# Router scores taken from the out-projection's own columns, normed rows on ScalarE, and a new order of the first expert tile

## The reference

```python
h = concat([tokens(x), txt], axis=1)              # (4, 384, 192)
# block: xn = layernorm(h); xz = xn @ in_proj_w.T; conv of 4 taps, silu -> u
#   dt = softplus(u @ dt_w.T + dt_b); state = exp(dt*A)*state + dt*B*u  (16 states); y = sum_n C_n*state_n
#   r = (y + D*u) * silu(z) @ out_w.T + xn
h = h + (r - mean(r)) / sqrt(var(r) + 1e-5) * ln_g + ln_b
# experts: xf = layernorm(h)
router_logits = xf @ Wr.T                         # 8 experts
topk_vals, topk_idx = top_k(router_logits, 2); w = softmax(topk_vals)
h = h + sum_k w_k * (gelu(xf @ Wi[e_k].T + bi[e_k]) @ Wo[e_k].T + bo[e_k])
```

## Time and profile before

| | us |
|---|---|
| median of 3 runs | 439.72 (438.59 to 440.37) |
| profiled execution | 440.68, of which the span 438.9 |
| TensorE busy | 375.9 (86%), mean granted clock 0.92 |
| VectorE busy | 275.1 (63%) |
| Pool busy | 224.3 (51%) |
| ScalarE busy | 197.8 (45%) |

### The profile page before, as it was taken

One profiled execution on the slowest core, in us unless ns is written; L12 is line 12 of the kernel. 1 busy time (PEld: TensorE's weight loads), 2 busy tenths in 40 slices (PEclk: granted clock), 3 DMA queues, 4 the chain that ended last, 5 costly groups with the idle time before them and its releaser, 6 DMA issues.

```text
span 438.9 us, 6787 instructions
## 1 busy us (share of the span) xinstructions
PE 375.9 (86%) x2247; PEld 281.5 (64%) x2247; DVE 275.1 (63%) x498; ACT 197.8 (45%) x502; POOL 224.3 (51%) x166
## 2 busy tenths in 40 slices
PE   5989897989849968879688698899999999999960
PEld 4546555644425535545355586699999999999960
DVE  4525479899899999999995566343443534435300
ACT  1455576566915565445550210135444454444420
POOL 6777732666546727576370003035565564655421
PEclk9998999799979978999699866699999999999995
DMA  6310015544637764989664411313323233233314
GB/s 174 67 12 4 7 24 132 120 114 125 136 92 233 239 219 144 261 236 292 182 184 175 197 37 41 127 23 54 56 43 56 48 51 54 42 55 50 38 21 117
DMA packets 36614, 46.97 MB, mean 107 GB/s; under 512 B 8877, under 2 KB 25214, under 8 KB 36014
## 3 DMA queue, kind: packets, MB, share of 16 engines
q1 hardware_dynamic: 29262, 38.94, 30.9%
q0 software_dynamic: 7328, 7.74, 11.7%
HBM read 40.65 MB, written 7.19 MB: 109 GB/s over the span
## 4 chain that ended last, share of the span: by engine, by line
PE 49%; DVE 17%; POOL 8%; DMA 7%; issue 6%; SPq 6%; ACT 4%; POOLq 0%; DVEq 0%; ACTq 0%
PE ps L1106 14%; PE ps L1089 10%; PE ps L1095 6%; DVE w_all L1620 5%; POOL w_all L664 4%; PE ps L852 4%; DMA w_all<-bc_dram 4%; SPq L530 3%; DVE ps L1612 3%; POOL w_all L614 2%; DMA sum_dram<-u_cm,tok_row 2%; DVE y_cm L1566 2%; PE ps L1079 2%; PE ps L919 2%; SPq L528 1%
## 5 line engine op out<-in xcount | busy, mean ns | idle before, releaser
L664 POOL TENSOR_TENSOR w_all<-w_all 128x768 f32<-128x768 f32 x47 | 78.9, 1680 | 73.0 <-DVE w_all L1620 27.4
L689 POOL DMA_INDIRECT sum_dram<-u_cm,tok_row x31 | 50.3, 1622 | 65.9 <-ACT u_cm L1441 59.5
L919 PE MATMUL ps<-w_all,cst 128*128 128x512 f32 x96 | 56.8, 675 | 22.5 <-POOL w_all L664 22.2
L1620 DVE TENSOR_TENSOR_SCAN w_all<-decay,ps 128x780 f32<-128x780 f32 x40 | 71.1, 1779 | 1.5 <-POOL w_all L664 0.2
L673 POOL DMA_INDIRECT dt_cm<-x_dram,tok_in x31 | 30.6, 986 | 51.4 <-DVE decay L1790 37.2
L614 POOL DMA_INDIRECT w_all<-in_pix,gidx x42 | 45.1, 1074 | 14.8 <-issue 12.5
L852 PE MATMUL ps<-cst 128*128 128x256 f32 x136 | 41.2, 463 | 5.6 <-DMA cst<-in_cst 5.0
L1426 ACT ACTIVATE u_cm<-ps,x_cm 128x128 f32<-128x128 f32 x96 | 26.6, 377 | 42.2 <-PE ps L1095 42.2
L1612 DVE TENSOR_TENSOR ps<-dtu_cm,ps 128x768 f32<-128x768 f32 x40 | 38.0, 949 | 2.9 <-PE ps L900 1.6
L919 PEld LDWEIGHTS ps<-w_all,cst 128*128 128x128 f32 x96 | 17.4, 208 | 34.3 <-POOL w_all L664 30.1
L852 PEld LDWEIGHTS ps<-cst 128*128 128x128 f32 x136 | 30.5, 232 | 13.4 <-DMA cst<-in_cst 5.0
(11 more groups left out here) (228 smaller groups left out, 686.4 us busy)
## 6 DMA issues: line engine op xcount, KB each, us to landing
w_all<-bc_dram SPq DMA_DIRECT2D x48, 256.0 KB, 3.6
w_all<-bc_dram SPq DMA_DIRECT2D x96, 64.0 KB, 3.7
w_all<-in_w_all SPq DMA_DIRECT2D x20, 289.0 KB, 4.2
w_all<-in_w_all SPq DMA_DIRECT2D x3, 1156.0 KB, 7.4
b_wide_sb<-bc_dram SPq DMA_DIRECT2D x8, 256.0 KB, 3.9
x_dram<-x_cm SPq DMA_DIRECT2D x3, 384.0 KB, 5.1
sum_dram<-h_tok SPq DMA_DIRECT2D x3, 384.0 KB, 3.5
out<-sum_dram SPq DMA_DIRECT2D x4, 288.0 KB, 3.8
```

Source lines behind the costliest of these rows:

```text
L664: nc.gpsimd.tensor_tensor(segments(hcs[at % 2]), inner(states[at % 2]), segments(c_sb[at % RING]), ALU.mult).then_inc(hc_rdy, 1)
L689: pool.indirect_dma_start(sum_dram, bass.IndirectOffsetOnAxis(ap=tok_row[:, i:i + 1].bitcast(U32), axis=0), y_out[:, i % 2, :], None, comp ...
L919: nc.tensor.matmul(sums[:, 0:4 * P], ident, hcs[at % 2][:, 0:4 * P], start=False, stop=at % S == S - 1, skip_group_check=True)
L1620: v.tensor_tensor_scan(states[p], fade, drive, 0.0, ALU.mult, ALU.add).then_inc(scanned, 1)
```

## The change

The last norm of a token is of h = h0 + (r - mean)*g/dev + b. Its shift and scale do not change which experts are largest. So the scores are built from parts: the router's weights less their mean over channels (`w_rt`, `w_b`), times g; the input's part (`token_rows`, from the transposed normed input), and the out-projection with 8 further columns that hold out_w times those weights (`mixed_weights`); `unscaled_scores` and `router_scores` put them together behind the first deviation alone. Only the difference of the two best is later scaled by the second deviation for the softmax. `router_rows` of VectorE, the transposes and logit matmuls of TensorE and ScalarE's copies for them go; ScalarE makes the normed rows in one instruction per tile from a scale and a shift (`row_shift`). The last chunk's out-projection goes to four banks and is signalled in two halves; new h and its statistics come behind the count. The gates are made behind the slots. Fillers are counted anew. Of the first expert tiles, the transposes of tile 1, the copies of weights and the stores' additions change order. The six added loads bring g and b with one channel per partition. The core of the diff:

```diff
+        N_TOK, N_IN, N_MIX = 11, 3, 12
         JS = [2, 0, 1]
 
         RUNS = [(2 * P + K - 1, L), (0, P), (P, 2 * P + K - 1)]
         NORMS = [(0, 2), (0, 0), (0, 1), (1, 0), (2, 0), (1, 1), (2, 1), (1, 2), (2, 2)]
-        WARM = {"input weights": 10, "coarse levels": 2, "fine patches": 4, "patches": 7, "normed rows": 7, "convolution": 2,
-                "first step": 12, "router's rows": 14, "counts": 6, "slots": 9, "bias rows": 2,
-                "first tile": 3}
+        WARM = {"input weights": 10, "coarse levels": 2, "fine patches": 2, "patches": 7, "normed rows": 7, "convolution": 2,
+                "first step": 10, "last rows": 11, "slots": 20, "bias rows": 1, "first tile": 4}
...
+        def attn_bank(j, b):
+            return 4 * (b % 2) + b // 2 if j == NJ - 1 else 4 + b // 2
+
+        def attn_rows(j, b):
+            at = 0 if j == NJ - 1 else 256 * (b % 2)
+            return ps[:, attn_bank(j, b), at:at + C + E]
...
+            by_channel = d["ln_gb"].rearrange("o g c -> c o g")
+            for k in range(2):
+                sp.dma_start(gb_c[:, 0, k:k + 1], by_channel[0:P, :, k]).then_inc(ld_mix, 16)
+                for half in range(2):
+                    sp.dma_start(gb_c[CB * half:CB * half + CB, 1, k:k + 1], by_channel[P:C, :, k]).then_inc(ld_mix, 16)
...
-                if at in (1, 5, 9):
-                    add_shift(at // 4)
+                if at in (1, 5, S + 2):
+                    add_shift(at // 4 if at < S else 2)
...
+            def router_weights():
+
+                pe.wait_ge(ld_mix, 16 * N_MIX)
+                pe.wait_ge(ones_set, 1)
+                pe.wait_ge(z_ready, 1)
+                nc.tensor.matmul(ps[:, 6, 0:E], ones_p, wr[:, 0, :], start=True, stop=False)
+                nc.tensor.matmul(ps[:, 6, 0:E], ones_p[0:CB, :], wr[0:CB, 1, :], start=False, stop=True)\
+                    .then_inc(w_sum_ps, 1)
+                for at, c in ((0, slice(0, P)), (256, slice(P, C))):
+                    o = ps[0:c.stop - c.start, 7, at:at + C]
+                    nc.tensor.matmul(o[:, 0:P], ow[:, 0, c], ident, start=True, stop=True)
+                    mm = nc.tensor.matmul(o[:, P:C], ow[0:CB, 1, c], ident[0:CB, 0:CB], start=True, stop=True)
+                mm.then_inc(owt_ps, 1)
+
+            def token_rows(n, bank, at):
+
+                for i in range(2):
+                    o = ps[:, bank, at + 4 * E * i:at + 4 * E * i + 4 * E]
+                    for half in range(2):
+                        b = 2 * half + i
+                        nc.tensor.matmul(o[:, 2 * E * half:2 * E * half + 2 * E], xt_a[:, P * b:P * b + P], w_rt[:, 0, :],
+                                         start=(half == 0), stop=False, skip_group_check=True)
+                    mm = nc.tensor.matmul(o, xt_b[:, P * i:P * i + P], w_two[:, :, :].rearrange("p h e -> p (h e)"),
+                                          start=False, stop=True, skip_group_check=True)
+                mm.then_inc(rows_ps, 1)
+
+            def first_rows():
+
+                pe.wait_ge(w_rt_step, 6)
+                pe.wait_ge(abs_rdy, 1)
+                pe.wait_ge(linear_rdy, 1)
+                for at, lo, hi in ((0, w_rt[:, 0, E:2 * E], w_rt[0:CB, 1, E:2 * E]), (E, w_b[:, 0, :], w_b[0:CB, 1, :])):
+                    nc.tensor.matmul(ps[:, 5, at:at + E], ones_p, lo, start=True, stop=False)
+                    nc.tensor.matmul(ps[:, 5, at:at + E], ones_p[0:CB, :], hi, start=False, stop=True)
+                token_rows(0, 5, 64)
+
+            def mixed_weights():
+
+                attn_free(0)
+                pe.wait_ge(owt_rdy, 1)
+                for o, ch in ((ps[:, 5, 0:E], slice(0, P)), (ps[0:CB, 5, E:2 * E], slice(P, C)),
+                              (ps[CB:P, 5, E:2 * E], slice(P, C))):
+                    nc.tensor.matmul(o, owt_a[:, ch], w_rt[:, 0, E:2 * E], start=True, stop=False)
+                    mm = nc.tensor.matmul(o, owt_b[:, ch], w_rt[0:CB, 1, E:2 * E], start=False, stop=True)
+                mm.then_inc(mixed_ps, 1)
...
             z_projection(0, 6)
             coarse_transposes()
-            keep_warm(WARM["coarse levels"], 4)
+            router_weights()
             coarse_levels()
-            pe.wait_ge(ld_mix, 16 * N_MIX)
             pe.wait_ge(x_out, 2)
             dt_low(0)
             dt_high_and_bc(0)
             coarse_rows()
             keep_warm(WARM["fine patches"], 0)
+            first_rows()
...
+            pe.wait_ge(abs_rdy, 3)
+            pe.wait_ge(linear_rdy, 3)
+            token_rows(1, 4, 0)
...
+            def last_residual_rows(i):
+
+                if i:
+                    attn_free(2)
+                else:
+                    pe.wait_ge(scanned, STEPS - 1)
+                for b in (i, 2 + i):
+                    nc.tensor.matmul(attn_rows(2, b), ident, xn[:, 2, b, :], start=True, stop=False, skip_group_check=True)
...
-                if i == 1:
+                if i == 1 or j == NJ - 1:
...
                 if n == 0:
                     if s == 1:
+                        filler(4)
                         fine_level(1)
...
                         pe.wait_ge(x_out, 6)
+                        token_rows(2, 4, 0)
                         z_projection(2, 4)
...
+                    elif s == 13:
+                        mixed_weights()
+                    elif s == S - 1:
+                        filler(12)
...
-                    elif s == 12:
-                        router_transposes(n - 1)
-                    elif s in (13, 14):
-                        router_logits(n - 1, s - 13)
-                    elif s not in (2, 4):
+                    elif at == STEPS - 2:
+                        last_residual_rows(1)
+                    elif s == 2:
+                        attn_free(n - 1)
+                        filler(3, 4)
+                    elif s == 8:
+                        filler(3)
+                    elif s != 4:
                         filler()
                 if at >= 2 and (n == 0 or s != 2):
                     sum_states(at - 2)
...
-            residual_rows(2)
             sum_states(STEPS - 1)
             for i in range(2):
+                if i == 0:
+                    last_residual_rows(0)
                 out_projection(2, i)
-            keep_warm(WARM["router's rows"], 0)
-            router_transposes(2)
-            for i in range(2):
-                router_logits(2, i)
-            keep_warm(WARM["counts"], 0)
+            keep_warm(WARM["last rows"], 7)
...
+                if not is_at_least(i, 1):
+                    x_transposed(1, 1)
...
+            def router_rows(j):
+
+                act.wait_ge(shift_rdy, j + 1)
+                for t in range(NB * j, NB * j + NB):
+                    ins = nc.scalar.activation(xf[:, t, 0:C], h_tok[:, j, t - NB * j, :], ACT.Identity,
+                                               bias=shift[:, t:t + 1], scale=rstd[:, 2, t:t + 1])
+                ins.then_inc(xf_rdy, 1)
...
+            def router_weights():
+
+                def wide_e(a):
+                    return a.rearrange("p (k o) -> p k o", o=1).to_broadcast([P, 2, E])
+
+                dve.wait_ge(ld_mix, 16 * N_MIX)
+                dve.wait_ge(w_sum_ps, 1)
+                v.scalar_tensor_tensor(w_rt[:, :, 0:E], ps[:, 6, 0:E].rearrange("p (o e) -> p o e", o=1)
+                                       .to_broadcast([P, 2, E]), -1.0 / C, wr[:, :, :], ALU.mult, ALU.add)\
+                    .then_inc(w_rt_step, 1)
+                dve.wait_ge(w_rt_step, 1)
+                v.tensor_tensor(w_rt[:, :, E:2 * E], w_rt[:, :, 0:E], wide_e(gb_c[:, :, 0]), ALU.mult).then_inc(w_rt_step, 1)
+                v.tensor_tensor(w_b[:, :, :], w_rt[:, :, 0:E], wide_e(gb_c[:, :, 1]), ALU.mult).then_inc(w_rt_step, 1)
+                v.memset(w_two[:, :, :], 0.0).then_inc(w_rt_step, 1)
+                dve.wait_ge(w_rt_step, 4)
+                for half in range(2):
+                    rows = slice(CB * half, CB * half + CB)
+                    v.tensor_copy(w_two[rows, half, :], w_rt[rows, 1, :]).then_inc(w_rt_step, 1)
...
+            def input_scores():
+
+                dve.wait_ge(rows_rdy, NJ)
+                v.tensor_tensor(p1[:, :, :], p1[:, :, :], std[:, 0, :].rearrange("p (t o) -> p t o", o=1)
+                                .to_broadcast([P, NT, E]), ALU.mult).then_inc(p1_step, 1)
+                dve.wait_ge(p1_step, 1)
+                v.tensor_tensor(p1[:, :, :], p1[:, :, :], b_sum[:, :].rearrange("p (o e) -> p o e", o=1)
+                                .to_broadcast([P, NT, E]), ALU.add).then_inc(p1_step, 1)
...
+            def unscaled_scores(j):
+
+                t = slice(NB * j, NB * j + NB)
+                scored(v.tensor_tensor(logit[:, t, :], per_tile(mv[:, 1, t, 0]), g_sum[:, :]
+                                       .rearrange("p (o e) -> p o e", o=1).to_broadcast([P, NB, E]), ALU.mult))
+                four = logit[:, t, :].rearrange("p (h i) e -> p h i e", h=2)
```

(80 more changed lines are left out.)

207 lines of the change are left out of this document (112 added, 95 removed).

## The result

The changed kernel takes 434.11 us (median of 4 runs, 431.38 to 435.86); the kernel before, run beside it, 439.15 (437.41 to 440.37). The ratio is 0.9895, 95% interval 0.9855 to 0.9936. So it is faster, by 5.0 us where 11.2 were forecast (439.72 to 428.5). The profiled execution took 433.38, of which the span 431.6; against the one of before the span is 7.3 shorter, so the search is for some 4 us that did not come.

What follows compares the result with a forecast made beforehand. VectorE was taken to bound the scan, TensorE the expert loop, and a chain between both the stretch between them. 440.7 - 10.6 - 1.6 - 1.7 + 2.5 = 429.3, less 1.0 for the median: 428.5 us, 8-in-10 range 423.5 to 436.5.

Steps and rivals of the forecast that it cites:

- Part 1: Tail after the scan: a shorter chain between TensorE and VectorE brings the first slot matmul earlier, gain 10.6 us.
- the first fetch waited: Sign of being wrong, at the first expert tile: the fetch starts over a microsecond after its token list.
- Part 2: First expert tiles: reordered transposes and copies close the hole ahead of the second tile's matmuls, gain 1.6 us.
- the rival of the early clock: Bias rows and first tile: TensorE keeps 2.4 GHz through them, giving 423.5 us; chance 0.11.
- Part 3: Scan: VectorE's work and waits change, sum -1.7 us, bounds -4 and +2.
- The wait of 1.62 at 80.78: Scan, step 1: four fillers replace a TensorE hole followed by half clock, for which VectorE waited; gain 1.2 us.
- The move on Pool: Scan: the shift of h moves from step 9 to 18 on Pool, gain 0.5 us, bounds 0 and 1.8.
- the term for SP: Scan: rows come about a step later and may hold the next broadcast up to 1 us, covered by three buffers.
- Part 4: Set-up: matmuls added to TensorE's queue cost +2.5 us, bounds +0.7 and +7.
- first rows: Set-up: ten small matmuls on TensorE, 2.4 us at full clock or 4.6 at half, against two fillers removed.
- the rival of a slow set-up: Set-up: half clock through its small matmuls and all seven fillers, +7 instead of +2.5, 433 us; chance 0.08.
- beyond 46: Sign of being wrong, in the set-up: first patch transposes stand beyond 46 us, where they stood at 41.55.

Runs made afterwards that it cites:

- e2: Changed kernel without the seven pairs of fillers ahead of the first patch transposes: 432.17 us, ratio 0.9809 to the kernel before.
- e9: The changed kernel timed once more, unedited: 435.33 us, ratio 0.9888 to the kernel before.
- e11: Changed kernel with the first chunk's choice of the best experts back at step 31: 431.53 us, ratio 0.9841 to the kernel before.
- e12: Changed kernel with rows sent a step later, one load for g and b, and four pairs of fillers in two TensorE waits: 429.61 us, ratio 0.9829.
- e8: Changed kernel with the second tile's transposes behind the whole first up-projection on TensorE: ratio 0.9878 to the kernel before.
- e15: Changed kernel with rows sent a step later, one load for g and b, and Pool's last add of b back at step 9: ratio 0.9834.
- e1: Changed kernel with SP sending a chunk's normed rows one step later: 431.35 us, ratio 0.9865 to the kernel before.
- e5: Changed kernel with rows sent a step later and one load for g and b: 468.66 us beside 476.87 of the kernel before, ratio 0.9807.
- e10: Changed kernel without the three pairs of fillers at step 2 of a chunk: 431.25 us, ratio 0.9827 to the kernel before.
- e17: Changed kernel with rows sent a step later, g and b from one load, and the six small loads into an unread tile: ratio 0.9887.
- e18: Changed kernel with rows sent a step later, six loads kept, and four pairs of fillers in two TensorE waits: ratio 0.9911.

## Why the prediction was wrong, point by point

**Part 1, the tail: right in size, wrong on the stores.** 31.95 to 21.76 us is 10.2 for 10.6, and every kernel with the old place of the send has 21.76 to 21.78. The first slot matmul stands 262.66 - 241.43 = 21.2 us behind the end of the second last sum, for "about 20". Score operations come every 0.21 to 0.23; the 20 pairs end ahead of VectorE by 0.85, for 0.8. But the first fetch waited, which the prediction had as a sign of being wrong: it starts 1.8 us behind the token list, where it was 0.3 before.

```profile
266.88 0.18 DVE L1980 TENSOR_SCALAR tok_in<-decay 128x31 int32<-128x31 f32 x1
...
268.85 0.97 POOL L706 DMA_INDIRECT dt_cm<-x_dram,tok_in  x1 [29.03 <-DVE texi L1989]
```

The profile names VectorE's `texi`, for which Pool does not wait. The last of the gates' stores was issued at 262.0 and took 6.1 us to land; the fetch starts 0.75 us behind that landing, and it is 0.75 or 0.76 in all 19 traces with the change. So the stores are what it waits for: 0.4 to 1.9 us after the token list. It was free all the same, since TensorE goes from its fillers to the first tile's transposes without a wait. ScalarE's next activation came 1.29 us after the start of the table load that its gates' exponential needs (258.17 and 256.88). The Trainium skill (ScalarE: Activation LUTs, section What ACT_TABLE_LOAD costs) would have a drain of 1.38 there besides the load; this trace, too, has no room for one.

**Part 2, the first tiles: the size right at equal clock, the place half wrong.** Where the first up ran at half clock, as it did before, the stretch was 18.5 to 19.1 (e2, e9, e11, e12), a gain of 1.8 to 2.4 for the forecast 1.6. In the first profile of the changed kernel it ran at full clock, 4.5, as in five of the nine traces with the change in the first table. That is the rival of the early clock in part only: the clock fell among the slot matmuls as before (at 264.8) and the bias rows ran at half, but it was back at 275, where before it came back at 284. TensorE's order gave only 0.5 of it (e8); the hole at 284.79 was VectorE's weights copy, which now stands ahead of the token copy.

**Part 3, the scan: the first step that failed.** -1.7 was forecast; it was +2.7 (+0.7 to +3.2 in other traces of the same scan). The wait of 1.62 at 80.78 went as said: the fourth product came 8.03 us behind the first instead of 9.73. The move on Pool gave 0 for 0.5 (e15). But the term for SP was put at nothing, and the sentence that SP's send "may hold the next broadcast by up to 1 us, covered by three buffers" was wrong: Pool waited 3 us and VectorE stalled for 2.24. The prediction counted the buffers, and neither the time of SP's queue nor that the change takes away, in the same steps, the work on VectorE that had let the queue catch up. Of the new place of the choice of the best experts (the argmax) it said nothing at all. With the send one step later the scan is 160.40, 0.5 under before; the forecast would have been 159.2. Most of what is left is the second chunk's argmax, which before took its 0.95 us behind the last product, where VectorE waited for TensorE anyway (1.77 us, until 235.66), and takes it inside the scan now. Its first instruction, before and after:

```profile
232.84 0.36 DVE L1657 MAX8 top_v<-logit 128x8 f32<-128x8 f32 x4
```

```profile
223.39 0.35 DVE L1822 MAX8 top_v<-logit 128x8 f32<-128x8 f32 x4
```

This is read from the two timelines; no run put it back.

**Part 4, the set-up: the second step that failed. The first rows' price was right, a term was missing, and the clock was wrong.** First rows 2.53 for 2.4, less two pairs of fillers at 0.43 each: +1.7 for +1.5. But at equal clock the set-up is 3.1 longer (the estimate above), because the coarse levels start 1.45 later, which the prediction had at nothing ("stand where TensorE waited"). The other 3.1 of the 6.2 is clock: (10.2 - 3.4) x 0.46. In five traces of one and the same set-up it was +4.6 to +9.2, with the clock at half for 6.8 to 17 us. This is the rival of a slow set-up, which had 0.08; it was the rule. The patch transposes at 47.79 are the sign that the prediction had named ("beyond 46"). Two statements fell with it: that the router's first matmuls stand in a wait (with the gather 0.8 later, they delayed the coarse levels from 23.20 to 24.65), and that what lies ahead of the fillers doesn't change the fillers' clock.

**The sum.** With the measured parts, 10.2 + 4.5 + 1.5 - 2.7 - 6.2 = 7.3. The time, 434.1, is in the range; the gain is 5.0 and not 11.2 because a new stall in the scan (3.2, by e1), a lower clock ahead of it (3.1, for some 1 in the forecast) and the later coarse levels (1.45, for nothing) came together. The first tiles gave 2.9 more than forecast, and that is luck: it hangs on where the clock returned in that execution. The kernel that takes stall and clock back, e12, gained 437.35 - 429.61 = 7.7, e5 8.2; none was measured at the whole 11.2.

## What to carry to other kernels

When a change takes work off the bounding engine, look at who was catching up behind that work: here a queue that issues one transfer each 0.5 us, and whose transfers landed over a microsecond later behind a store, had its slack there, and the buffers that seemed to cover it did not. An ordinary store goes behind the transfers that a step will wait for, not in front of them; that was one character, and 1.2 to 3.8 us. And price a chain of TensorE's fillers and small matmuls at both clocks, for the whole of it: one profiled execution shows one draw.

## What the runs showed of the hardware

The granted clock before the scan differed between executions of the same instructions: half clock for 6.8, 6.8, 6.8, 10.2 and 17.0 us in five traces, at different places (the 17.0 is from the slowest of e10's four executions). The spans follow the clock roughly: the changed kernel's four runs had 431.6 and 434.0 us at a mean clock of 0.941, 433.0 at 0.945 and 429.6 at 0.957.

In three of the five batches in which the experiments were timed every kernel, the one before too, took about 38 us longer (476 for 438). TensorE in the timeline of e5 shows where:

```profile
33.20 0.26 PE L786 MATMUL ps<-w_all 48*64 48x64 f32 x1 [1.59 <-issue]
35.32 0.26 PE L786 MATMUL ps<-w_all 48*64 48x64 f32 x1 [1.86 <-issue]
```

In the coarse levels TensorE stood for 1.2 to 3.2 us ahead of single matmuls, 25 us in all, without waiting for anything that the profile shows. The same chip was in this state in one batch and not in another (e17 and e18 against e9 to e12), so it is no property of a chip; the cause is open.
